# Moving the layer-norm transposes and the down projection to earlier helper steps in the scan of a two-layer kernel

## The reference, cut to what matters

```python
def step(h, inputs):                       # the scan, one token
    u_t, d_t, b_t, c_t = inputs
    dA = jnp.exp(d_t[..., None] * A)
    h = dA * h + (d_t * u_t)[..., None] * b_t[:, None, :]
    y = jnp.einsum('bdn,bn->bd', h, c_t)   # 128 channels, 64 states
    return (h, y)
...
up = y @ W_up + b_up                       # y: layer norm of x
left, right = jnp.split(up, 2, axis=-1)
left = silu(causal_dwconv(left))           # gives u; delta, B, C are products of u
gated = scan(left) * silu(right)
s = xn + gated @ W_down + b_down
...
x = x + s * silu(moe(xn))                  # 16 experts, top-k tokens, gelu(g) * u
```

## Time and profile before

| | |
|---|---|
| median of 3 runs | 4754.91 us (4753.7 to 4758.17) |
| the profiled execution, own time | 4758.17 us |
| its span, first to last instruction | 4756.4 us |
| layer 1, with the combine | from about 2160 us to the end |
| last recurrence of the scan ends | about 4709 us |

### The profile page before, as it was taken

How to read it: one execution, slowest core, us unless ns; L and a number is a source line. 1 busy time by engine, 2 the same in 40 slices (tenths; PEclk the granted TensorE clock), 3 DMA queues, 4 the chain that set the end, 5 groups by cost and what they waited for, 6 DMA issues and landing times. The chain is left out here.

```text
span 4756.4 us, 68001 instructions
## 1 busy us (share of the span) xinstructions
PE 4083.1 (86%) x24660; PEld 3380.9 (71%) x24660; DVE 3477.4 (73%) x4975; ACT 2579.2 (54%) x4869; POOL 2589.5 (54%) x1858
## 2 busy tenths in 40 slices
PE   8899999979999999978888866778888887888865
PEld 7788888858788888867777755656676666666653
DVE  5466666655566666626888889988888888888887
ACT  6544444437444444447576653256667666666655
POOL 3122222223122210026666656878999899999887
PEclk9999999989999999979999967889999999999996
DMA  2022222221122210024444431255655556556658
GB/s 90 19 97 76 85 86 76 88 87 41 52 89 73 88 58 20 22 68 141 148 143 140 141 112 60 81 173 167 192 178 179 176 186 188 173 172 190 188 164 315
DMA packets 271490, 572.90 MB, mean 120 GB/s; under 512 B 37169, under 2 KB 157746, under 8 KB 271154
## 3 DMA queue, kind: packets, MB, share of 16 engines
q1 hardware_dynamic: 246578, 534.98, 33.7%
q0 software_dynamic: 24576, 33.57, 3.9%
HBM read 445.64 MB, written 122.81 MB: 120 GB/s over the span
## 5 line engine op out<-in xcount | busy, mean ns | idle before, releaser
L1595 POOL TENSOR_TENSOR scan_drive_sb<-scan_b_wide_sb,scan_du_sb 128x1024 f32<-128x1024 f32 x512 | 1299.8, 2565 | 269.5 <-DVE scan_h_sb L1507 262.6
L1507 DVE TENSOR_TENSOR_SCAN scan_h_sb<-decay_bank,scan_state_sb,scan_drive_sb 128x512 f32<-128x512 f32 x896 | 1116.2, 1268 | 114.7 <-ACT decay_bank L1845 108.8
L1845 ACT ACTIVATE decay_bank<-scan_delta_sb,a_neg_sb 128x512 f32<-128x512 f32 x1024 | 701.0, 687 | 382.1 <-DVE scan_h_sb L1507 378.9
L1012 PE MATMUL ybank<-v_low_hi_lo_sb,pt_hi_b_sb 128*128 128x384 f32 x2048 | 665.6, 359 | 26.9 <-DVE pt_lo_b_sb L884 20.8
L1514 DVE TENSOR_TENSOR scan_ch_sb<-c_pair,scan_h_sb 128x1024 f32<-128x1024 f32 x512 | 614.2, 1200 | 63.6 <-PE c_pair L1682 63.3
L884 DVE TENSOR_TENSOR pt_lo_b_sb<-pt,pt_hi_b_sb 128x512 fp32r<-128x512 f32 x512 | 352.7, 690 | 420.1 <-ACT pt_hi_b_sb L1058 420.1
L1693 PE MATMUL y_bank<-identity_sb,scan_ch_sb 128*128 128x128 f32 x4096 | 652.2, 291 | 5.1 <-ACT scan_temp_sb L1863 5.1
L1693 PEld LDWEIGHTS y_bank<-identity_sb,scan_ch_sb 128*128 128x128 f32 x4096 | 546.2, 152 | 118.4 <-issue 19.1
L1682 PE MATMUL c_pair<-scan_cc_sb,select_state_sb 128*128 128x512 f32 x1024 | 387.1, 462 | 259.7 <-DVE scan_ch_sb L1514 259.0
L1049 ACT ACTIVATE p_b_sb<-scores,softmax_cols_b_sb 128x1024 f32<-128x1024 f32 x256 | 286.0, 1117 | 546.3 <-DVE softmax_cols_b_sb L878 409.1
L1013 PE MATMUL ybank<-v_low_hi_lo_sb,pt_lo_b_sb 128*128 128x256 f32 x2048 | 573.7, 280 | 0.0
(11 more groups left out here) (328 smaller groups left out, 9898.6 us busy)
## 6 DMA issues: line engine op xcount, KB each, us to landing
scan_b_wide_sb<-b_scratch SPq DMA_DIRECT2D x512, 512.0 KB, 3.9
w_hi_scratch<-split_hi_sb SPq DMA_DIRECT2D x51, 512.0 KB, 2.8
w_lo_scratch<-split_lo_sb SPq DMA_DIRECT2D x51, 512.0 KB, 4.1
expert_hi_sb<-w_hi_scratch SPq DMA_DIRECT2D x48, 512.0 KB, 5.4
expert_lo_sb<-w_lo_scratch SPq DMA_DIRECT2D x48, 512.0 KB, 6.4
x_b_sb<-x SPq DMA_DIRECT2D x16, 512.0 KB, 4.0
split_raw_sb<-WgT SPq DMA_DIRECT2D x16, 512.0 KB, 5.5
x_res_b_sb<-x SPq DMA_DIRECT2D x64, 128.0 KB, 4.9
```

The source lines that it names most:

```text
L1012: e.matmul(k.y_bank[:, 0:D + P], k.pt_hi[n % 2][:, cols], kv.v[:, block, :], start=(kb == 0), stop=False, skip_group_check=True)
L1507: e.tensor_tensor_scan(k.h[i % H_BUFFERS][:, j, :], k.decay_banks[S % DECAY_BANKS][:, :], k.drive[i % DRIVE_BUFFERS][:, j, :], start, ALU. ...
L1595: e.tensor_tensor(k.drive[i % DRIVE_BUFFERS][:, :, :], k.b_wide[i % B_BUFFERS][:, :, :], k.du[c % 2][:, :].unsqueeze(1).broadcast_to([P, P ...
L1845: e.activation(k.decay_banks[S % DECAY_BANKS][:, :], k.delta[c % 2][:, :], ACT.Exp, scale=wt.a[:, n:n + 1]).then_inc(k.s_decay, 1)
```

## The change

Three step tables are changed. `turned` goes from steps 11 and 13 of `prepare` to 10 and 11, `down_pair` from steps 8 and 10 of `down` to 7 and 9, and `down` has 12 steps instead of 13.

```diff
-TURNED_AT = (11, 13)
+TURNED_AT = (10, 11)
...
-PAIRS_AT = (8, 10)
-DOWN_STEPS = 13
+PAIRS_AT = (7, 9)
+DOWN_STEPS = 12
```

## The result

| | before | changed |
|---|---|---|
| median of 4 runs, us | 4756.54 (4753.7 to 4760.72) | 4789.82 (4784.8 to 4793.53) |
| span of the profiled execution, us | 4756.4 | 4790.1 |

The ratio is 1.0067, 95% interval 1.0054 to 1.008. The changed kernel takes 33 us more; 4753 was predicted, within 4732 to 4770.

The account below looks back on a forecast made before the run. DVE's loop of two recurrences and one read_out was taken to set the pace; terms -6, 0, +3, +2, 0 and +0.5 made -0.5 us, rounded to -2, giving 4753 us against the 4754.9 median, range 4732 to 4770.

Parts of the forecast that it names:

- Down pair: DVE's residual waiting for PE's pair at L1524: waits fall from 26 to 20 us, -6 us.
- Turned: DVE's waits at L1460: one Gelu collision less, -5 us, offset by tighter first halves and ACT's shorter lead; sum 0.
- C's lower part: Its step in prepare goes to a first half, waiting 0.2 to 0.6 us each at L1479: +3 us.
- Broadcast C: PE's C, awaited at L1514, late where one item holds too many fills: +2 us, between -10 and +15.
- Decay: DVE's waits for ACT's decay banks, mostly caused by Gelu steps that don't move: 0, with 10 us to either side.
- the three come to 53.2 us: DVE's helper waits at L1524, L1460 and L1479, 1.1% of the time, taken as all held up directly by the moved steps.
- The end: Last chunk, where SP's queued stores change order and DVE idles for loads: moves by 0.5 us, at most 1.5.
- B: Rival: first halves too tight, PE and ACT miss the deadline at L1460 and L1479; +20 us, 4775; chance 0.15.
- C: Rival: Silu, logarithm and Gelu loads meet in other chunks; 10 to 15 us either side, 4742 or 4768; chance 0.12.
- A: Rival: slack worth more, most of the residuals' 26.0 us go; some -20 us, 4735; chance 0.25.

Follow-up runs that it names:

- e13: The changed kernel itself, measured once more: ratio 1.0057 to the kernel before, 4786.67 us.
- e12: Kernel before with down pairs at steps 9 and 11 and down of 14 steps, so prepare comes one half-item later: 0.9998, 4764.05 us.
- e6: Kernel before with down of 14 steps only, so prepare of chunks 2 to 15 comes one half-item later: 0.9984, 4751.51 us.
- e9: Repeat of e2, kernel before with only the down pairs moved to steps 7 and 9: 1.0023, 4770.19 us.
- e2: Kernel before with only the down pairs moved to steps 7 and 9, down keeping 13 steps: 1.0047, 4778.3 us.
- e1: Kernel before with only turned moved to steps 10 and 11: 0.999, 4755.99 us.
- e14: Repeat of e3, the changed kernel with turned left at steps 11 and 13: 1.0034, 4775.49 us.
- e10: Kernel before with turned at 10 and 11 and prepare of chunks 2 to 15 one half-item earlier, pairs left alone: 1.0017, 4769.95 us.
- e5: Kernel before with prepare of chunks 2 to 15 one half-item earlier by its empty step 2, down untouched: 1.0016, 4766.6 us.
- e15: Changed kernel with ACT's exponentials of the logits issued one half-item earlier in the experts' block: 1.0032 to the kernel before, 4775.82 us.
- e4: Kernel before with turned at 10 and 11 and pairs at 7 and 9, down keeping 13 steps: 1.001, 4764.65 us.
- e3: Kernel before with pairs at 7 and 9 and down of 12 steps, turned left at 11 and 13: 1.005, 4782.05 us.
- e11: Kernel before with turned at 10 and 11 and down of 14 steps, pairs left at 8 and 10: 0.9972, 4748.49 us.
- e16: e11 with ACT's exponentials of the logits one half-item earlier, as in e15: 0.9972 to the kernel before, 4743.02 us.
- e8: Changed kernel with DVE's sum of delta and C's lower part one half-item later: 1.0092 to the kernel before, 4801.76 us.

## Why the prediction was wrong, point by point

**Down pair, -6: wrong, and this is one of the two steps that failed.** "PE comes 1.8 us earlier, but DVE's slot comes 1.2 us earlier too" gave 20 us for L1524; it is 26.5 (26.7 in e13). The arithmetic took PE's new slot as given by the old trace and moved nothing else. It put the pair "ahead of the expert fill of 1.47 us", and left out what that does to the fill: it and the C behind it are later. What the runs show in its place is some 10 us of L1514 in two items of the chunk, in every version with the pairs in first halves, and a cost of 7 us (e12 against e6), 11 (e9) or 22 (e2) instead of a gain of 6.

**Turned, 0: right alone, not in company.** e1 measured 5 us faster. L1460 came out at 21.4 us where I said near 20, the waits of over 3 us now in chunks 1, 8 and 11 and no longer in 2 and 13, as worked out from the tables. But the sum took for granted that an effect is the same in any company. Where pairs and shift are present (e13 against e14), `turned` at the new place costs 0.0057 - 0.0034, 11 us. About half of it lies in the scan (2569.2 against 2563.6 us). One piece shows: it adds a third wait of PE for the exponentials, 6.4 us against 4.7. But it does so in e10 too, and e10 is no slower than e5; the cause stays open.

**C's lower part, +3: right in kind, half in size.** +6.4 us at L1479. DVE's sum of delta (L1474), which changes halves just as C does, wasn't in the sum at all: +10.4. I had counted the steps where DVE waits for PE or ACT, and missed that this one waits for POOL. Only the view of waits has its row, and it was small before.

**Broadcast C, +2: the total is right by two errors.** L1514 went from 63.3 to 64.4. Against e10 (53.6), which is the change without its pairs, it is +11 from the pairs, and the shift and `turned` gave -10 (55.5 in e5, 52.4 in e1). "I counted the fills of every item" missed the second as well. Why the pairs alone raise the total by only 0.7 (e2) or 3.4 (e9), with 10 us more behind the pairs, isn't shown.

**Decay, 0 with 10 to either side: just at its bound.** -10.3 us, and it belongs to the shift: 12 us less in e5 and in e6.

**The experts' waits: the other step that failed; they weren't in the sum.** I wrote that "every helper step meets another step of theirs" and then priced only the scan's own instructions, by taking "the three come to 53.2 us" for "all that is held up directly". The order of the ring is common to both pipelines, so a helper of the scan can hold up a gate product. L2380 +19.2 and L2399 +4.2 are three quarters of DVE's net loss over the rows above: 1.1 + 0.5 + 0.1 + 6.4 + 10.4 + 19.2 + 4.2 - 10.3 = 31.6 us, while the scan took 26.5 longer. What was taken away and measured of it is the logits' bank, 11 us (e15).

**The end, +0.5: right that it hardly moves.** 48.3 and 48.1 us, although DVE's last wait for the loads is 8.2 us where it was 7.01.

**"No instruction is added or taken away":** true of what the program writes, but two more table loads of ACT came with the new halves. At 1.28 us each they are small beside the rest.

**The rivals.** B had the sign and a size that was near, +20, by luck. Its own mark, 1.5 us or more at nearly every second turned_lower, shows in 3 of chunks 2 to 15 in the changed kernel, and L1460 as a whole didn't move; with all halves changed in e6, the kernel is faster. C said that meetings with the Gelus could go either way by 10 to 15 us; they are meetings with the experts' fills that did so. A, that most of L1524's 26.0 us would go, never came near.

Measured against each other, by the ratios times 4757 us:

| pairs / shift / turned | us |
|---|---|
| turned (e1) | -5 |
| shift (e5) | +8 |
| pairs (e2, e9) | +22, +11 |
| pairs, turned (e4) | +5 |
| shift, turned (e10) | +8 |
| pairs, shift (e3, e14) | +24, +16 |
| all (the change, e13) | +32, +27 |
| shift the other way (e6) | -8 |
| that and turned (e11) | -13 |

The pairs lose in every company. So does the shift, but on top of the pairs alone only by 1 us in the ratios of one round (e3 against e2), though by 15 us or more in the lengths of the scan. Entries that differ by 5 to 11 us and come from two rounds can't be told apart. The version that beats both kernels is e11, and e16 with it: 0.9972, 13 us faster than before.

What stays open: the 11 us of `turned` in company, which meetings other than the logits' make the direction of the shift count, the spread of e2, and whether the pair's residual could be had cheaper with PE's order left alone: to empty that bank a half-item later would hold the ring as in e8, and wasn't tried.

## What to carry to other kernels

Where two pipelines share a ring of banks and in-order engines, price a moved step by what then stands behind it in the ring and on the engine that empties it, those of the other pipeline above all. Look in the trace for banks whose emptying waits behind an unrelated helper, and move that first: here it gave 11 us, more than was hoped for from the steps themselves, in the version that had such waits, and nothing in the one that hardly had any. Such a shift should be tried in both directions: the same steps moved by half an item cost 8 us one way and gave 8 the other.

## What the runs showed of the hardware

A wait of PE can cost twice. After the 1.44 us wait at 2348.41 the first matmuls of 256 columns take 0.28 us as before it, and from 2349.03 on 0.42. Windows of the changed kernel, columns as in the earlier trace rows, ahead of that wait and behind it:

```profile
2340.00:2347.00 7.00, 6.98 (x43) 5.37 (x41) 4.96 (x5) 5.96 (x10) 6.30 (x4) 1.00 0.44 150
2348.90:2352.40 3.50, 3.50 (x17) 3.25 (x16) 1.65 (x2) 1.58 (x5) 1.71 (x1) 0.51 0.18 58
```

The granted clock is 1.00 (2.4 GHz) while PE is busy all the time, and 0.51 (1.2 GHz nearly throughout) behind the wait, although PE is busy for all of those 3.50 us; C was issued in this stretch and took 1.11 us instead of the 0.62 of the one at 2343.57. So the matmuls behind a stall can be slow just where DVE waits for them.

It isn't so behind every wait. In the scan of the changed kernel PE idled 77 times for 1 to 1.5 us from a stretch at full clock, and the clock fell in or within 3 us behind only 7 of these. Nor is this stretch a cost of the change: in the kernel before, the clock there was 0.50 for longer, 2342.3 to 2349.1, behind a wait of 2.05 us. Around the 2.90 us wait the clock was low twice, 2417.2 to 2420.6 and 2424.0 to 2427.4; the first time began ahead of the wait, with PE busy since 2406.45.

In the whole scan the low stretches come to 468 us before and 529 after. How much of the loss that is can't be said from these runs: PE's busy time differs between executions too (4102.5 us in e13 against 4114.3 for the same kernel, and 4065.2 in e10, which is slower than the kernel before with its 4083.1).

The Trainium skill ("TensorE: Matmul & The Clock Gate", A second HAM failure mode: psum-queue depth-cycling) tells of PE idling briefly between groups of matmuls as it cycles through PSUM banks, so that the clock goes back and forth between its two levels; the trace agrees in that the clock falls behind some of these waits and comes back. It also advises ("Perfetto Trace Analysis", Matmuls) to rotate independent groups through different banks, so that the emptying of one overlaps the next. This kernel does, and the rows at 2418.91 to 2425.94 show that it isn't enough: the overlap holds only if the emptying instruction doesn't stand behind one that waits for the next group.
